# Group statistics of x read per image during attention, as 128 contiguous partitions, in place of one pass ahead of it

## What is computed

```python
def _gn(v, G=32, eps=1e-5):
    g = v.reshape(B_, G, C_ // G, H_, W_)
    m = jnp.mean(g, axis=(2, 3, 4), keepdims=True)
    s = jnp.var(g, axis=(2, 3, 4), keepdims=True)
    return ((g - m) / jnp.sqrt(s + eps)).reshape(v.shape)

# layer 0: windows of 16 x 16 pixels, 8 heads of 12 channels, linear attention
qkv = jnp.einsum('oc,bchw->bohw', w_qkv, x)       # x is the normalised one
q = _l2norm(q).transpose(0, 1, 3, 2); k = _l2norm(k)
tailor = 1.0 / (ws * ws + jnp.einsum('bhnc,bhc->bhn', q, k.sum(axis=-1) + EPS))
kv = jnp.einsum('bhmn,bhcn->bhmc', k, v)
attn = (jnp.einsum('bhnm,bhmc->bhcn', q, kv) + v.sum(axis=-1, keepdims=True)) * tailor
y = jnp.einsum('oc,bchw->bohw', w_proj, out)      # then batch norm over (0, 2, 3)

x = x + _L0_conv_ref(_gn(x), ...)                 # attention
x = x + _L1_conv_ref(_gn(x), ...)                 # 5 x 5 and wavelet convolutions
```

## Time and profile before

| | us |
|---|---|
| median of three runs | 11901.09 (11895.07 to 11904.0) |
| the profiled execution | 11889.79 |
| its span, first to last instruction | 11888.0 |
| PE busy | 10743.1 (90%) |
| DVE busy | 9364.9 (79%) |
| ACT busy | 6980.0 (59%) |
| POOL busy | 3393.1 (29%) |

### The profile page before, as it was taken

One profiled execution on the slowest core, in us unless ns is written; L12 is line 12 of the kernel. 1 busy time (PEld: TensorE's weight loads), 2 busy tenths in 40 slices (PEclk: granted clock), 3 DMA queues, 4 the chain that ended last, 5 costly groups with the idle time before them and its releaser, 6 DMA issues. The chain is left out here.

```text
span 11888.0 us, 209663 instructions
## 1 busy us (share of the span) xinstructions
PE 10743.1 (90%) x68680; PEld 9231.7 (78%) x68680; DVE 9364.9 (79%) x16196; ACT 6980.0 (59%) x11653; POOL 3393.1 (29%) x2756
## 2 busy tenths in 40 slices
PE   0006999999999999999969999999999999999999
PEld 0005888888888888888858888888888888888888
DVE  6667888888888888888867777777777777777777
ACT  0005888888888888888844444555554444444554
POOL 1002444444444444444421222222222222222221
PEclk9999999999999999999979999999999999999999
DMA  9993222222222222222236666666666666666665
GB/s 233 217 219 88 80 80 78 82 75 85 75 85 75 85 75 79 81 76 84 75 76 147 147 147 149 149 148 148 149 149 149 147 147 147 147 147 147 149 149 125
DMA packets 1149490, 1452.08 MB, mean 122 GB/s; under 512 B 202079, under 2 KB 1111711, under 8 KB 1111967
## 3 DMA queue, kind: packets, MB, share of 16 engines
...
...
## 5 line engine op out<-in xcount | busy, mean ns | idle before, releaser
L1076 PE MATMUL ps_w<-zb,mat 128*128 128x512 f32 x4800 | 1925.5, 401 | 0.1
L1078 PE MATMUL ps_w<-zb,mat 128*128 128x512 f32 x4800 | 1907.8, 397 | 0.0
L1077 PE MATMUL ps_w<-zb,mat 128*128 128x512 f32 x4800 | 1907.2, 397 | 0.0
L1029 ACT ACTIVATE z<-x,prm 64x384 f32<-64x384 f32 (+1 forms) x3072 | 1806.3, 659 | 54.7 <-DVE x L1139 47.0
L491 POOL CAST xn_hi<-xs 96x512 fp32r<-96x512 f32 x1024 | 882.6, 862 | 2854.7 <-PE ps_qkv L515 2067.2
L975 POOL CAST mat<-raw 128x1280 fp32r<-128x1280 f32 (+1 forms) x288 | 344.1, 1213 | 4452.5 <-DMA raw<-vec 2641.1
L1201 DVE SCALAR_TENSOR_TENSOR ob<-ps_w,prm,x 64x512 f32<-64x512 f32 x1920 | 1440.3, 750 | 182.6 <-PE ps_w L1119 143.6
L1139 DVE SCALAR_TENSOR_TENSOR x<-yb,prm,xb 128x1024 f32<-128x1024 f32 (+1 forms) x576 | 1120.7, 1997 | 387.0 <-DMA prm<-params 341.2
L513 PE MATMUL ps_qkv<-wqkv_hi,xn_hi 96*128 96x288 f32 x4096 | 1383.7, 338 | 23.3 <-POOL xn_lo L493 20.0
L493 POOL TENSOR_TENSOR xn_lo<-xs,xn_hi 96x512 fp32r<-96x512 f32 x1024 | 1297.8, 1267 | 82.2
L1049 ACT ACTIVATE ll<-ps_ll 128x512 f32<-128x512 f32 x192 | 115.1, 599 | 1882.7 <-PE ps_ll L1084 1882.7
...
## 6 DMA issues: line engine op xcount, KB each, us to landing
xs<-in_x SPq DMA_DIRECT2D x256, 1536.0 KB, 9.1
y_scratch<-ys SPq DMA_DIRECT2D x128, 1536.0 KB, 9.3
out<-ob SPq DMA_DIRECT2D x768, 208.0 KB
...
raw<-vec SPq DMA_DIRECT2D x192, 320.0 KB, 5.3
raw<-vec SPq DMA_DIRECT2D x384, 160.0 KB, 4.1
xb<-in_x SPq DMA_DIRECT2D x192, 240.0 KB
```

The source lines that it names most:

```text
L1029: last = nc.scalar.activation(z[q * WROWS:(q + 1) * WROWS, ts, b, :], x1[slot(k, g)][rows, pairs, b, q::2], ACT.Identity, scale=prm[k][row ...
L1076: mm(out_, w[HI], xx[HI], start=start, stop=False)
L1077: mm(out_, w[HI], xx[LO], start=False, stop=False)
L1078: return mm(out_, w[LO], xx[HI], start=False, stop=stop)
```

## The change

The first block now reads only image 0. It is read as 128 partitions of 49152 contiguous floats, three quarters of a channel each: four partitions hold three channels, that is one group. The image comes in 12 pieces of 128 x 4096 floats (2.10 MB) through four buffers. DVE first builds three small matrices from the identity (`same_grp`, `to_grp`, `to_chan`), then runs 8 bn_stats a piece, 96 in all, and the fold: three bn_aggr, one for each third of a partition (a third lies in one channel), means of a group by two small matmuls, deviations, variances by four small matmuls, root, scales. The result goes to a table `xpar` with eight numbers per image and channel, from which ACT's normalise reads.

In the second block the statistics of image b + 1 are taken while image b goes through the attention, for b = 0 to 6. SP issues one piece per strip, two strips ahead, between the store and the load; DVE runs one more bn_stats at the end of every step in the first 12 of an image's 16 strips. In the last four strips the fold is spread out: merge after step 4 of the first, the means in step 3 of the second, the variances in step 3 of the third, the root in step 5 and the scales in step 7 of it. PE's small matmuls write the bank that project_y writes too, so PE waits there until DVE has copied them out. The loops are nested now (image, strip), with image 0 and image 7 apart.

```diff
 NV2 = 2 * 2 * TAPS
 NPAR = 2 + 2 * B
+XP = 8
+PARTS = 128
+FLAT = C * H * W // PARTS
+STATS = 12
+PIECE = FLAT // STATS
+CHUNKS = PIECE // 512
 
 
...
+        def count_x(f, i, piece):
+
+            nc.vector.bn_stats(f.stat[:, i * STAT:(i + 1) * STAT], piece).then_inc(f.counted, 1)
+
...
+        def merge(dve, f, image):
+
+            v = nc.vector
+            link = linker(dve, f, image, 0)
+            third = STATS * CHUNKS * STAT // 3
+            dve.wait_ge(f.counted, (image + 1) * (STATS * CHUNKS))
+            dve.sem_inc(f.gathered, 1)
+            for j in range(3):
+                last = v.bn_aggr(f.mv[:, j, :], f.stat[:, j * third:(j + 1) * third])
+            link(last)
+            v.tensor_reduce(f.sums[:, 0:2], f.mv[:].rearrange("p j t -> p t j"), AX.X, ALU.add).then_inc(f.merged, 1)
+
+        def group_means(pe, f, ps, image):
+            pe.wait_ge(f.merged, image + 1)
+            nc.tensor.matmul(ps[:, 0:8], same_grp[:], f.sums[:], start=True, stop=True)
+            nc.tensor.matmul(ps[0:C, 8:16], to_grp[:], f.sums[:], start=True, stop=True).then_inc(f.means, 1)
+
+        def deviations(dve, f, ps, image):
+            v = nc.vector
+            link = linker(dve, f, image, 1)
+            dve.wait_ge(f.means, image + 1)
+            link(v.tensor_copy(f.gp[:], ps[:, 0:1]))
+            link(v.tensor_copy(f.cur[:, 2:3], ps[0:C, 8:9]))
+            link(v.tensor_scalar(f.parts[:, :, 0], f.mv[:, :, 0], f.gp[:], None, ALU.subtract))
+            link(v.tensor_tensor(f.parts[:, :, 1], f.parts[:, :, 0], f.parts[:, :, 0], ALU.mult))
+            link(v.tensor_tensor(f.parts[:, :, 1], f.parts[:, :, 1], f.mv[:, :, 1], ALU.add))
+            v.tensor_reduce(f.dsum[:], f.parts[:].rearrange("p j t -> p t j"), AX.X, ALU.add).then_inc(f.devs, 1)
+
+        def group_vars(pe, f, ps, image):
+            pe.wait_ge(f.devs, image + 1)
+            nc.tensor.matmul(ps[0:C, 16:24], to_grp[:], f.dsum[:], start=True, stop=True)
+            for j in range(3):
+                last = nc.tensor.matmul(ps[0:C, 24:32], to_chan[:, j, :], f.parts[:, j, :], start=j == 0, stop=j == 2)
+            last.then_inc(f.gvars, 1)
+
+        def spread_vars(dve, f, ps, image):
+            v = nc.vector
+            link = linker(dve, f, image, 6)
+            dve.wait_ge(f.gvars, image + 1)
+            v.tensor_scalar(f.tot[:, 0:1], ps[0:C, 17:18], GN_EPS, None, ALU.add).then_inc(f.eps_added, 1)
+            link(v.tensor_copy(f.cur[:, 5:7], ps[0:C, 24:26]))
+            link(v.tensor_tensor(f.cur[:, 0:1], f.cur[:, 2:3], f.cur[:, 5:6], ALU.add))
+            link(v.tensor_tensor(f.cur[:, 7:8], f.cur[:, 5:6], f.cur[:, 5:6], ALU.mult))
+            link(v.tensor_tensor(f.cur[:, 1:2], f.cur[:, 6:7], f.cur[:, 7:8], ALU.subtract))
+
+        def root(act, f, image):
+            act.wait_ge(f.eps_added, image + 1)
+            nc.scalar.activation(f.tot[:, 1:2], f.tot[:, 0:1], ACT.Sqrt).then_inc(f.rooted, 1)
+
+        def scales(dve, f, image):
+            v = nc.vector
+            link = linker(dve, f, image, 10)
+            dve.wait_ge(f.rooted, image + 1)
+            link(v.reciprocal(f.cur[:, 3:4], f.tot[:, 1:2]))
+            link(v.scalar_tensor_tensor(out=f.cur[:, 4:5], in0=f.cur[:, 2:3], scalar=-1.0, in1=f.cur[:, 3:4],
+                                        op0=ALU.mult, op1=ALU.mult))
+            v.tensor_copy(xpar[:, bass.ds(image * XP + first_image[0], XP)], f.cur[:]).then_inc(f.kept, 1)
+
...
             def _(sp):
-                with sp.Fori(0, B) as b:
-                    with sp.Fori(0, STRIPS_IMG // 2) as h:
-                        for k in range(2):
-                            sp.wait_ge(x_used[k], b * (STRIPS_IMG // 2) + h + 1)
-                            sp.dma_start(xs[:, k, :], x_strips[bass.ds(b, 1), bass.ds(h * 2 + k, 1)].squeeze()
-                                         ).then_inc(x_in[k], 16)
+                for i in range(STATS):
+                    if i >= XA:
+                        sp.wait_ge(fold.counted, (i - XA + 1) * CHUNKS)
+                    sp.dma_start(xst[:, i % XA, :], x_flat[0, :, i * PIECE:(i + 1) * PIECE]).then_inc(x_in[i % XA], 16)
 
...
-                nc.tensor.matmul(ps_m[:, 0:B], gmean_sb[:], mean_x[:], start=True, stop=True).then_inc(gmeans, 1)
-                pe.wait_ge(vars_, 1)
-                nc.tensor.matmul(ps_v[:, 0:B], gmean_sb[:], tot[:], start=True, stop=True).then_inc(gvars, 1)
+                pe.wait_ge(grouped, 1)
+                group_means(pe, fold, ps_f, 0)
+                group_vars(pe, fold, ps_f, 0)
...
-                        dve.wait_ge(x_in[k], (h + 1) * 16)
-                        for j in range(STRIP // 512):
-                            last = v.bn_stats(stat_x_all[:, bass.ds((h * 16 + (k * 8 + j)) * STAT, STAT)],
-                                              xs[:, k, j * 512:(j + 1) * 512])
-                        last.then_inc(x_used[k], 1)
-                for k in range(2):
...
-                link(v.scalar_tensor_tensor(out=nb0[:], in0=gm0[:], scalar=-1.0, in1=r0[:], op0=ALU.mult, op1=ALU.mult))
+                v.memset(to_chan[:], 0.0)
+                link(v.memset(fold.sums[:], 0.0))
+                link(v.memset(fold.parts[:], 0.0))
+                dve.wait_ge(const_in, 32)
+                link(v.tensor_reduce(blocks[:], ident_sb[:].rearrange("p (a r) -> p a r", r=4), AX.X, ALU.add))
+                for r in range(4):
+                    link(v.tensor_scalar(same_grp[:, r::4], blocks[:], 1.0 / 12, None, ALU.mult))
+                for i in range(3):
+                    link(v.tensor_scalar(to_grp[:, i::3], blocks[:], 1.0 / 12, None, ALU.mult))
+                for j in range(3):
+                    for r in range(4):
+                        part = to_chan[:, j, (3 * r + j) // 4::3]
+                        link(v.scalar_tensor_tensor(out=part, in0=ident_sb[:, r::4], scalar=0.25, in1=part,
+                                                    op0=ALU.mult, op1=ALU.add))
+                dve.sem_inc(grouped, 1)
+                for i in range(STATS):
+                    dve.wait_ge(x_in[i % XA], (i // XA + 1) * 16)
+                    for e in range(CHUNKS):
+                        count_x(fold, i * CHUNKS + e, xst[:, i % XA, e * 512:(e + 1) * 512])
+                merge(dve, fold, 0)
+                deviations(dve, fold, ps_f, 0)
+                spread_vars(dve, fold, ps_f, 0)
+                scales(dve, fold, 0)
 
...
-                        step(n, k, j, n * PAIRS + j)
+                            step(b, m, k, j, None if first is None else first + k * PAIRS + j, extra, stats)
+
+                body(0, 0, first=0)
+                with eng.Fori(1, BODIES - 1) as m:
+                    body(0, m)
+                body(0, BODIES - 1, extra=True, stats=False)
+                with eng.Fori(1, B - 1) as b:
+                    with eng.Fori(0, BODIES - 1) as m:
+                        body(b, m)
+                    body(b, BODIES - 1, extra=True, stats=False)
+                with eng.Fori(0, BODIES - 1) as m:
+                    body(B - 1, m, stats=False)
+                body(B - 1, BODIES - 1, first=LAST - XS * PAIRS, stats=False)
                 for j in range(PAIRS):
-                    step(STRIPS, 0, j, LAST + j)
+                    step(B, 0, 0, j, LAST + j, False, False)
 
             @block.sync
...
+                def load_piece(b, i, k):
+                    n = b * STATS + i
+                    if k is not None:
+                        sp.wait_ge(fold.counted, (n - 1) * CHUNKS)
+                    sp.dma_start(xst[:, (k or 0) % 2, :],
+                                 x_flat[bass.ds(b + 1, 1), :, bass.ds(i * PIECE, PIECE)].squeeze()
+                                 ).then_inc(xst_in[(k or 0) % 2], 16)
+
+                def body(b, m, pieces):
                     for k in range(XS):
-                        store(m * XS + k, k)
-                        sp.wait_ge(xy_counted, (m * XS + k + 1) * 4)
-                        load(m * XS + (k + XS), k)
-                for k in range(XS):
-                    store(STRIPS - XS + k, k)
+                        n = b * STRIPS_IMG + m * XS + k
+                        store(n, k)
+                        if pieces[k] is not None:
...
-                                  ).then_inc(xn_ready, 1)
+                    s_.activation(part, part, ACT.Identity, scale=xpar[:, bass.ds(b * XP + 3, 1)],
+                                  bias=xpar[:, bass.ds(b * XP + 4, 1)]).then_inc(xn_ready, 1)
 
                 def copy_att(u, first):
...
@@ -464,7 +604,11 @@
                     if j % 2 == 0 and inside_(at, -PAIRS) and (at is None or at < LAST - PAIRS):
                         if j == 0:
                             act.wait_ge(x_in[(k + 1) % XS], (n + 1) // XS * 16 + 16)
+                        if j == 0 and extra and k == XS - 1:
+                            act.wait_ge(fold.kept, b + 1)
```

(56 more changed lines are left out.)

179 lines of the change are left out of this document (106 added, 73 removed).

## The result

| | us |
|---|---|
| before, median of four runs beside the new one | 11898.15 |
| after, median of four runs | 11313.05 (11311.75 to 11319.26) |
| ratio | 0.9508 (95% interval 0.9495 to 0.9522) |
| predicted | 11332 (11190 to 11455) |
| span of the profiled execution | 11309.9, before 11888.0 |

What follows compares the result with a forecast made beforehand. DVE and DMA were taken to bound the kernel up to 967.7 us, PE afterwards. 11888 - 821 (stage 1) + 17 (loop start) + 192 (bn_stats) + 43 (folds) = 11319 span, 11332 us as median; range 11190 to 11455.

Steps and rivals of the forecast that it cites:

- Stage 1: First block, before attention: 12 pieces replace 128 strips, so it ends at 147 us in place of 967.7, saving 821 us.
- The end at 135 to 150 us: Sign named for the forecast being right: stage 1 ending between 135 and 150 us.
- The stall by the pads' stores: In stage 1: the pads' stores delay the loads of x by 8.3 us, moving the last landing to 133.0 us.
- Loop start: Start of attention: queued strips and pieces hold DVE's first bn_stats, and PE waits for rk behind it; +17 us once.
- The bn_stats of x: Attention loop, 672 steps: one more bn_stats makes khat late in odd steps, worsened by POOL's cast; +192 us over 84 strips.
- A step 7 that loses most: Sign named for the forecast being wrong: step 7 of a strip losing more than the other steps.
- The folds: Last strips of images 0 to 6, without new bn_stats: seven folds at 5.9 to 6.1 us each, +43 us (28 to 63).
- The merge: Part of each fold: three bn_aggr and a reduce behind an even step, 2.8 us less 0.34 of slack, 2.5.
- No exclusion: Rival, attention's odd steps: POOL's cast and the khat product do not block each other; 77 us not 192, 11217; chance 0.20.
- DVE saturates: Rival, attention loop: DVE's idle time stays and each bn_stats adds its 0.60 us; 403 not 192, 11543; chance 0.08.
- It all hides: Rival, attention loop: the bn_stats cause no PE delay; 11140 us; chance 0.06.
- Late pieces: Rival, attention loop: pieces taking over 35 us delay every strip and make the kernel slower, 12170 at 38 us; chance 0.03.

Runs made afterwards that it cites:

- the other place: Kernel after with the even steps' x bn_stats moved into the odd step, behind the khat product (L796): 11129.7 us, 183 less than 11313.
- the run with POOL's wait: Kernel after with one more wait on POOL, so its cast starts only when the khat product (L796) is done: 11182.3 us, 131 less.
- the run with loops alone: Kernel after without the attention loop's x bn_stats, the pieces' loads and the seven folds, only the new loop shape left: 11061.7 us.

## Why the prediction was right, point by point

**Stage 1: mechanism right, size off by 37 us.** The term that failed is the transfer: 9.1 us a piece, from the 230 GB/s of strips of 96 partitions. The pieces came 5.2 us apart (landings at 8.7, 14.0, 19.0 and 24.5 us). From this the two times that stood on it follow: the constants were there at 25.4 and not 40.6, and DVE with 4.8 us a piece set the pace in place of a DMA with 9.1. The end at 135 to 150 us that was named as a sign was therefore wrong, 109.5. The tail was right, 8.2 us from 101.2 to 109.4 against 8.6 forecast (its chain has fifteen small DVE operations, not seventeen). The stall by the pads' stores was foreseen, but too small: DVE waits 13.4 us beside them where 8.3 were allowed. The lesson lies in how the bound was taken: a rate of one shape of transfer was carried to another, with the DMA engines 95% busy as the reason to think it a limit. Busy engines were not a limit of bytes.

**Loop start: mechanism right, 5 us too high.** 12 us (53.4 for the first strip, 41.2 before) for 17. DVE was held by its first piece and PE by khat, as said:

```profile
146.38 0.69 DVE L871 BATCH_NORM_STATS2 f_stat_b<-xst 128x6 f32<-128x512 f32 x1 [13.54 <-DMA xst<-in_x]
...
147.97 0.67 PE L688 MATMUL ps_g<-tok 128*104 128x97 f32 x2 [11.01 <-DVE tok L796]
```

The strips came 6.8 to 7.2 us apart, as taken, but the piece landed 4.6 us behind the last of them and not 9.1: the same term as in stage 1. Not in the prediction was the clock: it is granted at 0.50 from 140.1 to 153.7 us, in PE's 11.01 us of idle time and behind it. What share of the 12 us that is was not separated.

**The bn_stats of x: right, and shown.** 192 us forecast, 84 times 2.4 = 202 in the strips, 183 got back by the other place and 196 by leaving them out. The 196 hold the 12 us of the first strip, which the prediction had as a term of its own; strip by strip the bn_stats cost 188 against the kernel without them. The two parts were separated by the run with POOL's wait: 0.25 to 0.34 us of plain lateness a step (0.26 forecast), the rest from the cast standing ahead. Steps 1, 3 and 5 lost 0.62 each (0.66 forecast); step 7 went from a distance of 1.73 us to 2.30 and lost 0.57, not 0.3. There the prediction had seen both requests fall on the same instant and had taken a middle value between 0.03 and 0.58; POOL won. So 3 x 0.62 + 0.57 = 2.43 us a strip stand against the 2.28 forecast, two small errors in opposite directions. A step 7 that loses most was listed as a sign of being wrong, and it did not show: step 7 ends latest of the four, but it did so before the change too, and it loses least.

**The folds: the sum right, its parts not.** 43 forecast; their own three strips gave 45, the run without them 56. The merge was taken at 2.5 us; without a fall of the clock it costs 2.6 (42.2 us in image 1), but in six of seven images PE's wait of 2.3 us is followed by half clock and it costs 4.2 to 5.6. The two strips with small matmuls cost 1.0 and 1.2 and not 1.5 and 1.9. That these make up for each other is luck.

**The term that was missing: the jumps of the loops**, 26 us by the run with loops alone and by the one with the image loop written out. The change section named the nested loops, the timeline of the kernel before has 1.2 us more in one strip of four, and the prediction gave the jumps no term. By the strips the loss is the five ends of images, where PE jumps together with the rest and mostly starts at half clock. The inner jumps became dearer by the exclusion that DVE's late return sets off, but there are half as many, and these two cancel.

**Rivals.** No exclusion: out, by L796's length and by the run that removed the exclusion alone. DVE saturates: out, since the same work elsewhere costs 12 us. It all hides: out, by PE's new wait. Late pieces: a piece lands 13.8 us after its issue in the median, far from the 28 at hand, and DVE waits for one only in the first step.
